# Ninety-five unread TensorE products in the waits of a fused attention and feed-forward block

## The reference, cut to what matters

```python
def _act_fake_quant(x, clip_factor):
    scale = jax.nn.sigmoid(clip_factor) * jnp.max(jnp.abs(x)) / QMAX
    return jnp.clip(_ste_round(x / scale), -QMAX - 1.0, QMAX) * scale
...
    xq = _act_fake_quant(x, clip_x[0])
    gate = jnp.einsum('bsh,ih->bsi', xq, _weight_fake_quant(w_gate))
    up = jnp.einsum('bsh,ih->bsi', xq, _weight_fake_quant(w_up))
    h = _act_fake_quant(jax.nn.silu(gate) * up, clip_down[0])
    return jnp.einsum('bsi,hi->bsh', h, _weight_fake_quant(w_down))
...
x = x + jnp.tanh(g_xattn[0]) * _L0_xattn_ref(_layernorm(x, axis=-1), ctx_1024, ctx_1024, ...)
x = x + jnp.tanh(g_ffn[0]) * _L0_ffn_ref(_layernorm(x, axis=-1), ...)
```

## Time and profile before

| | |
|---|---|
| median of 3 runs | 291.31 us (288.94 to 291.93) |
| profiled execution | 290.14 us, of which the span of the trace 288.3 us |
| TensorE busy, products | 234.4 us, 81% |
| VectorE busy | 214.7 us, 74% |
| ScalarE busy | 175.6 us, 61% |
| GpSimd busy | 124.2 us, 43% |
| mean granted TensorE clock | 0.95 |

### The profile page before, as it was taken

How to read it: one execution, slowest core, us unless ns; L and a number is a source line. 1 busy time by engine, 2 the same in 40 slices (tenths; PEclk the granted TensorE clock), 3 DMA queues, 4 the chain that set the end, 5 groups by cost and what they waited for, 6 DMA issues and landing times.

```text
span 288.3 us, 6469 instructions
## 1 busy us (share of the span) xinstructions
PE 234.4 (81%) x1784; PEld 157.3 (55%) x1788; DVE 214.7 (74%) x468; ACT 175.6 (61%) x327; POOL 124.2 (43%) x210
## 2 busy tenths in 40 slices
PE   1699886988978999999999999999851588853990
PEld 1587775866745675657666675655530233322650
DVE  3479889775477879796988879798327569997991
ACT  1325486366586767576675777577941478866940
POOL 3375655433361315253443615254405777430472
PEclk9999999999999999999999999999996599995896
DMA  7839899973335544435345455000000700000298
GB/s 237 236 82 333 237 264 281 268 169 113 109 109 114 110 113 109 106 72 108 60 105 110 110 110 110 2 1 3 1 3 8 249 0 2 0 0 0 33 127 135
DMA packets 31638, 31.28 MB, mean 108 GB/s; under 512 B 5248, under 2 KB 28288, under 8 KB 31616
## 3 DMA queue, kind: packets, MB, share of 16 engines
q1 hardware_dynamic: 26832, 27.87, 38.4%
q0 software_dynamic: 1904, 1.84, 5.2%
q10 hardware_dynamic: 2880, 1.31, 1.7%
HBM read 20.65 MB, written 10.22 MB: 107 GB/s over the span
## 4 chain that ended last, share of the span: by engine, by line
PE 41%; DVE 24%; issue 14%; ACT 6%; DMA 5%; POOL 5%; DVEq 1%; POOLq 1%; ACTq 0%; SPq 0%
PE bank_a L1260 6%; PE bank_o L1277 6%; PE bank_m L1303 5%; PE bank_b L1247 5%; DVE neg_max L795 4%; PE bank_a L1169 4%; PE bank_b L1400 3%; PE bank_o L1180 2%; PE bank_m L1285 2%; DMA big<-in_ctx 2%; DVE arena L1072 2%; PE bank_m L1293 2%; DVE h_max L1032 2%; DVE x_rows L894 2%; PE bank_a L1400 1%
## 5 line engine op out<-in xcount | busy, mean ns | idle before, releaser
L795 DVE TENSOR_REDUCE neg_max<-bank_b 128x2 f32<-128x512 f32 x112 | 73.8, 679 | 10.9 <-PE bank_b L1247 10.9
L656 ACT ACTIVATE big<-bank_a 128x512 f32<-128x512 f32 x128 | 69.6, 589 | 15.0 <-PE bank_a L1260 14.5
L1260 PE MATMUL bank_a<-big 98*128 98x256 bf16 x256 | 49.0, 273 | 2.9 <-DMA big<-max_parts 1.4
L1247 PE MATMUL bank_b<-big 96*128 96x256 bf16 x224 | 42.8, 272 | 0.0
L1277 PE MATMUL bank_o<-big,v_cur 128*32 128x256 f32 x512 | 34.3, 385 | 0.8 <-ACT big L656 0.8
L1169 PE MATMUL bank_a<-arena,w_t 128*128 128x256 f32 x128 | 30.8, 390 | 0.6 <-DVE resid L806 0.5
L476 POOL CAST max_parts<-max_f 8x256 bf16<-8x256 f32 x16 | 6.5, 406 | 56.1 <-ACT max_f L614 49.8
L1260 PEld LDWEIGHTS bank_a<-big 98*128 98x128 bf16 x256 | 21.2, 97 | 13.2 <-ACT big L656 3.1
L1169 PEld LDWEIGHTS bank_a<-arena,w_t 128*128 128x128 f32 x128 | 24.2, 197 | 4.1 <-DVE resid L806 1.0
L449 POOL TENSOR_TENSOR arena<-resid,arena 128x512 bf16<-128x512 f32 x16 | 18.4, 1160 | 18.5 <-ACT arena L595 18.5
L1247 PEld LDWEIGHTS bank_b<-big 96*128 96x128 bf16 x224 | 21.5, 97 | 3.2 <-DVE neg_max L795 0.2
(11 more groups left out here) (161 smaller groups left out, 464.6 us busy)
## 6 DMA issues: line engine op xcount, KB each, us to landing
qk_parts<-arena SPq DMA_DIRECT2D x8, 768.0 KB, 5.2
big<-qk_parts SPq DMA_DIRECT2D x32, 192.0 KB, 3.8
big<-qk_parts SPq DMA_DIRECT2D x32, 128.0 KB, 4.0
x_rows<-in_x SPq DMA_DIRECT2D x8, 256.0 KB, 5.2
big<-qk_parts SPq DMA_DIRECT2D x32, 64.0 KB, 4.0
out<-x_rows SPq DMA_DIRECT2D x8, 256.0 KB, 3.1
big<-in_ctx SPq DMA_DIRECT2D x7, 256.0 KB, 6.6
out<-v_all POOLq DMA_DIRECT2D x7, 256.0 KB, 4.6
```

The lines of the kernel that those rows point to most:

```text
L656: act.activation(p_buf[:, h % HH], bank_a[:, h % 2].rearrange("p (c s) -> p c s", c=QC), ACT.Exp, scale=SCALE).then_inc(exp_done, 1)
L795: dve.tensor_reduce(neg_max[:, p, :, h], bank.rearrange("p (c s) -> p c s", c=QC), axis=AX.X, op=ALU.max, negate=True).then_inc(max_done, 1)
L1247: done = mm(to, q_st[0:KR, p, h, c * P:(c + 1) * P], k_st[0:KR, p, h], start=True, stop=not masked)
L1260: done = mm(to, k_st[0:KM, p, h, k * P:(k + 1) * P], q_st[0:KM, p, h], start=True, stop=not masked)
```

## The change

A helper `keep_busy(n, moving, bank)` issues n products of the identity with some moving operand into a bank that nobody reads before it is written anew. It is called at eight places: in the prologue 16, 6 and 12 products of 128 columns, in the chain to the gate products 5, 12, 11 and 5 products of 512 columns, and in the chain to the last stage 14 and 14 of 512 columns. That is 34 narrow and 61 wide products. The moving operand of the wide ones is a part of `mask_bias`. A wait on the last silu is added ahead of the last call; it stands behind a wait for the maximum, which comes later.

```diff
+            def keep_busy(n, moving, bank):
+                for _ in range(n):
+                    mm(bank, ident_b[:], moving, start=True, stop=True)
...
+            keep_busy(16, ident_b[:], bank_b[:, 3, 0:P])
             weight_tr(0)
             weight_tr(1)
+            keep_busy(6, ident_b[:], bank_b[:, 3, 0:P])
             x_tr(0, 0, 0)
             pe.wait_ge(w_ready, 1)
             weight_tr(2)
+            keep_busy(12, ident_b[:], bank_b[:, 3, 0:P])
             x_tr(1, 1, 0)
...
+            wide = mask_bias[:, 0:QC].rearrange("p t s -> p (t s)")
+            keep_busy(5, wide, bank_b[:, 3])
             pe.wait_ge(*used)
...
             spread(bank_o[:, E:E + P], PSUM_).then_inc(diag_done, 1)
+            keep_busy(12, wide, bank_b[:, 3])
             pe.wait_ge(wq_ready, 10)
             pe.wait_ge(amax_part, 1)
             spread(bank_m[:, 0:P], TMP).then_inc(amax_spread, 1)
             pe.wait_ge(wd_scale_ready, 1)
+            keep_busy(11, wide, bank_b[:, 3])
...
             xq_transpose(0)
+            keep_busy(5, wide, bank_b[:, 3])
...
             gate_up(NCH - 1, ahead=False)
+            keep_busy(14, wide, bank_m[:])
             pe.wait_ge(amax_part, 2)
             spread(bank_m[:, 0:P], TMP2).then_inc(amax_spread, 1)
+            pe.wait_ge(silu_done, NCH * IC + 3)
+            keep_busy(14, wide, bank_b[:, 3])
```

## The result

The changed kernel takes 292.46 us (median of 20 runs, 291.16 to 294.46), the kernel before 289.17 us (median of 20 runs, which include the three shown ahead). The ratio is 1.0105 (1.0081 to 1.0128): slower by about 3 us, where 3 us less was forecast. The forecast was added up from 291.31 us, the median of three runs; from the median of the twenty it would have started 2.1 us lower. The profiled execution took 294.46 us, with a span of 292.7 us against 288.3 before.

The account below looks back on a forecast made before the run. TensorE's clock, halved in dips around the chains to the gate products and last stage, was taken to delay the kernel. Gains 0.2 + 0.4 + 2.2 + 0.2 = 3.0 us turned 291.31 into 288.3 us; range 286.2 to 291.2.

Parts of the forecast that it names:

- Gain 0, cost 0: Prologue: the 16, 6 and 12 narrow fills are all hidden in waits, so they neither gain nor cost time.
- Twelve run from 217.12: Chain to the gate products: twelve wide fills take 2.6 us, to 219.7, leaving 0.9 us spare before the spread at 220.64.
- the rivals: Four other outcomes: chain alone gains (290.5 us, 0.14), clock falls (299.3, 0.08), loads don't hide (290.4, 0.06), more (286.8, 0.10).
- The clock falls in spite of the fills: Rival, both chains: fills run at 0.43 us each and delay what follows by 8.0 us, giving 299.3 us; chance 0.08.
- I take it that the clock stays at 1.00: Chain to the gate products: with fills, TensorE's longest wait is some 1.6 us, so its clock stays full.
- chain to the gate products 0.6 forecast: Before the first gate product: spread gains 0.2 us and transposes 0.4 us, so it loads at 227.0 instead of 227.60.
- Chunk 0: First gate products: twelve products take 2.6 us at full clock instead of 4.8, gaining 2.2 us more.
- the bound of 2.4 us: Gate stage: GpSimd's last division would end at 238.0 instead of 240.43, which would hold the stage's gain to 2.4 us.
- Second chain: Chain to the last stage: the spread falls from 0.47 to 0.27 us, gaining 0.2 us.
- The last five fills: Chain to the gate products: five fills run 1.1 us behind the transposes, with about 0.5 us spare before the first load.
- The weight loads: Every fill: its load was taken to hide; the rival that loads don't hide cost 2.1 us, giving 290.4; chance 0.06.
- The clock is already full there: Prologue: four fp32 transposes take 0.88 us from start to start, so fills there have no clock to raise.

Follow-up runs that it names:

- e1: Changed kernel with all six calls of wide products taken out, only the prologue's 34 narrow products left; 291.9 us against 289.61 before, ratio 1.011.
- e9: Kernel before plus 33 never-executed products in the attention branch not taken, and the second chain's added wait; 291.87 us against 289.91, ratio 1.0061.
- e10: Changed kernel with all its products, plus one never-executed product in the attention branch not taken; 287.1 us against 289.91 for the kernel before, ratio 0.9911.
- e2: Changed kernel without the prologue's three calls, only the 61 wide products left; 287.39 us against 289.61 before, ratio 0.9942.
- e6: Changed kernel with all 95 products, plus 94 never-executed products in the attention branch not taken; 287.02 us against 289.81 before, ratio 0.9901.
- e7: Changed kernel without the prologue's products, plus 17 never-executed products in the attention branch not taken; 286.97 us against 289.81 before, ratio 0.9898.
- e4: Changed kernel with only the two calls of 14 wide products in the chain to the last stage; 289.7 us against 289.61 before, ratio 1.0015.
- e5: Kernel before, no executed fills, plus 34 never-executed products in the attention branch not taken; 289.54 us against 289.81, ratio 0.9992.
- e8: Changed kernel without the twelve wide products in the chain to the gate products; 290.87 us against 289.81 for the kernel before, ratio 1.0028.

## Why the prediction was wrong, point by point

**The step that failed** is "Gain 0, cost 0" for the prologue's fills and, in the first chain, "Twelve run from 217.12". Each fill was priced by the time that it takes and by the gap that covers it. What it does to the place of the instructions behind it was not priced at all. The prologue's 34 products, called hidden, are what made the kernel slower (e1), not by running, but by the 67 places by which they move the rest (e9, e10). The 3.0 us pause was nowhere in the sum. None of the rivals was this one. A smaller slip lies in the same line: the first five fills, put at nothing, push the weight-scale product back even without the pause (2.4 us after L894 in e10, 1.5 before), so that the twelve start 2.9 us after L894 and not 2.2, and of the 0.9 us spare for them about 0.2 is left (12 x 0.22 from 217.68 is 220.3, the spread stands at 220.49). "The clock falls in spite of the fills" had one of its effects, fills 0.43 us apart that hold up the spread, but in the other order of cause: no load starts on TensorE between 218.18 and 221.18 us, and the clock fell at 219.1, within that pause. Its own condition did not hold: in e2, e6, e7 and e10, without the pause, the clock stays at 1.00 through the fills of both chains.

**"I take it that the clock stays at 1.00"** was right once there is no pause: e7 has nothing but 9 in its clock row until the last slice, e10 in both chains.

**The terms**, with the pause removed (e10 against before): chain to the gate products 0.6 forecast, 0.65 measured (12.71 to 12.06). Chunk 0, 2.2 forecast, 1.8 measured (32.78 to 30.98). In the changed kernel VectorE's second slice starts 3.58 us after the first gate load (234.02, 237.60) instead of 5.40, and GpSimd's last division ends at 245.02, 11.00 us after that load instead of 12.83: both 1.8 us earlier. VectorE waits nowhere in this stage of e10 for GpSimd, which the forecast had as the bound of 2.4 us. Most of the missing 0.4 us is in ScalarE's silus. The first two start 0.87 us apart, not 0.6, since the second waited for its gate bank:

```profile
234.75 0.69 ACT L732 ACTIVATE arena<-bank_b,w_scale_x 128x512 f32<-128x512 f32 x1 [1.16 <-PE bank_b L1412]
...
235.62 0.69 ACT L732 ACTIVATE arena<-bank_b,w_scale_x 128x512 f32<-128x512 f32 x1 [0.18 <-PE bank_b L1412]
...
237.60 0.75 DVE L1041 SCALAR_TENSOR_TENSOR big<-bank_a,w_scale_x,arena 128x512 f32 x1 [1.25 <-ACT arena L732]
```

Second chain 0.2 forecast, 0.15 measured; last stage 0 forecast, 0.26 in this pair (26.15 to 25.89), a stretch that lies between 25.4 and 26.3 us in all twelve profiles and does not follow the fills there: e4, with them, has 25.51 us, the changed kernel 26.11, e9, without them, 25.71. The four together are 2.9 us; the runs of e10 give 2.6 us. So the sum of 3.0 was right within 0.4 us for a kernel that the change missed by one instruction (a shift of 68 has no pause in e5) or two (69, e10). The last five fills had 0.3 us spare by the sum's own rows (1.02 + 0.41 - 1.1), not 0.5; in e10 it is 0.88 us from the end of their loads to the first gate load, so nothing hung on it.

**The weight loads** hide: the 13 recorded fills ahead of the second spread take 2.97 us from the first start to the last end, at most 0.23 us each. With the load of the earlier trace rows behind each product it would be 0.31. The rule weighed from the Trainium skill ("TensorE: Matmul & The Clock Gate", Part 3, The mechanism) says that such a load does not overlap; the trace doesn't agree.

**The prologue.** "The clock is already full there" was wrong. The record says 1.00, but four fp32 transposes take 1.06 us there, and 0.60 us later, in the kernel before:

```profile
14.18 1.06 PE L1133 MATMUL bank_b<-ident_f,big 128*128 128x128 f32 x4
...
21.98 0.60 PE L1133 MATMUL bank_b<-ident_f,big 128*128 128x128 f32 x4
```

In the changed kernel four such transposes take 0.60 us already at 10.87, and the first query products end earlier: ScalarE's first copy of them starts at 16.41 instead of 18.02 us. It gave nothing. The next transposes wait for VectorE's normalised rows (L785) and start at 21.67 us, before at 21.48. So the result, no gain, stood for another reason: not a full clock, but VectorE and GpSimd behind TensorE. e7, without the prologue's fills, and e10, with them, are equally fast.

## What to carry to other kernels

Work put into an engine's gaps is not free because it fits: it also moves every later instruction of that engine, and right behind a branch over much code, as here, one place can cost 3 us. Where a change adds instructions ahead of a critical stretch, look for "issue" between two instructions without a wait, and run once with a few never-executed instructions as padding before judging the change. Give fills a margin for a late start and for the lower clock too: twelve that fit in e10 cost 1.9 us in the changed kernel, 1.1 of it by starting late and 0.8 by the clock.

## What the runs showed of the hardware that was not expected

- TensorE's program comes in pieces of 16 KB. In windows of 0.2 us two of them stand out around the branch that leaves the attention. The second sets off 3.0 to 3.4 us after the first in all twelve profiles, with a pause or without (215.6 and 218.8 us in the changed kernel, 213.6 and 216.6 in e10). In the changed kernel the first load behind the branch starts at 218.18 and the first behind the pause at 221.18, both some 2.4 us after a piece sets off; in the five kernels with a pause the time from the second piece to the end of the pause is 2.2 to 2.8 us. If the first piece ends within two instructions of the target, there is a pause of about 3 us (3.00 us in the changed kernel, 3.01 in e8, 3.29 in e9); in e7, where by the shift it ends 34 instructions on, there is none. That the pieces are cut at fixed places of the program is shown by e5, e9 and e10, with shifts of 68, 66 and 69; why the second one is not asked for earlier stays open.
- Early in the execution the granted clock in the record can be 1.00 while products start twice as far apart as at full clock (0.22 against 0.11 us for an fp32 transpose). The times of the products are the safer sign.
- A fall of the clock during the projections comes and goes between the profiles. In slice 5 (the changed kernel from 38.2 us, e6 from 38.4) it costs: L894 starts at 216.85 and 216.59 us there, against 214.41 to 215.10 in the kernel before, e1, e2, e4, e7 and e8, which have no fall up to there. In slice 3 the cost is not clear: L894 starts at 213.98, 214.75 and 216.15 us in e5, e10 and e9. Whether the fills in the prologue change how often it comes was not settled.
